# A state-space mixer with a quantized feed-forward layer: the preparation in a new order, with five weight scalings and a new form of normalization on POOL

## The reference

```python
# x: 4 x 512 x 512; ctx: 4 x 512 x 256
def mixer(ctx, z, ...):                      # per batch, E = 512 channels, 16 states
    x = einsum('ed,bld->bel', in_proj_w, ctx)
    u = silu(causal_conv4(x, conv_w) + conv_b)          # depthwise, 4 taps
    dt_lo, B, C = split(einsum('ke,bel->bkl', x_proj_w, u))
    delta = softplus(einsum('er,brl->bel', dt_proj_w, dt_lo) + dt_proj_b)
    state = state * exp(delta * A) + (delta * u) * B    # a scan over 512 steps
    y = sum_n(state * C) + D * u
    return (y * silu(z)).swapaxes(1, 2)

def bit_linear(x, w):                        # activations to 8 bits, weights to -1, 0, 1
    s = 1 / clip(mean(abs(w)), 1e-5)
    qw = clip(round(w * s), -1, 1) / s
    return einsum('bsh,oh->bso', activation_quant(x), qw)

x = x + mixer(ctx, layernorm(x))             # z is the normalized x
h = silu(bit_linear(layernorm(x), w_gate)) * bit_linear(layernorm(x), w_up)
x = x + bit_linear(rms_norm(h, ln_weight), w_down)
```

## Time and profile before

| what | value |
|---|---|
| time, median of 3 runs | 574.37 us (573.48 to 574.68) |
| profiled execution, its span (first to last instruction) | 572.7 us |
| busy: PE / DVE / ACT / POOL | 536.1 / 535.1 / 513.3 / 465.1 us |
| first scan starts | 93.42 us |
| DMA moved | 68.64 MB |

### The profile page before, as it was taken

The page is one execution under the profiler, slowest core; times in us unless marked ns, Lnnn a source line. Parts: engine busy times, 40 slices in busy tenths (PEclk is TensorE's granted clock), DMA queues, the critical chain, the costliest instruction groups (busy, mean ns, idle before and its releaser), DMA issues.

```text
span 572.7 us, 10285 instructions
## 1 busy us (share of the span) xinstructions
PE 536.1 (94%) x3667; PEld 403.2 (70%) x3684; DVE 535.1 (93%) x778; ACT 513.3 (90%) x757; POOL 465.1 (81%) x196
## 2 busy tenths in 40 slices
PE   5888988899999999999999889999899999999996
PEld 2335477799998999989899879998344444444443
DVE  3999988999999999999999999999999999999883
ACT  1899999999999999989999899999987878878784
POOL 4889364999999999999999999995757676675772
PEclk9999999999999999999999998999999999999999
DMA  9992591221111832126632257443544344533521
GB/s 279 408 390 76 201 323 36 55 58 57 56 56 56 191 105 93 56 65 123 165 99 63 59 129 188 137 154 97 83 78 96 76 101 84 110 84 71 106 55 74
DMA packets 62194, 68.64 MB, mean 120 GB/s; under 512 B 41137, under 2 KB 41137, under 8 KB 59969
## 3 DMA queue, kind: packets, MB, share of 16 engines
q1 hardware_dynamic: 59776, 63.59, 37.5%
q0 software_dynamic: 2368, 4.40, 4.8%
HBM read 50.02 MB, written 8.52 MB: 102 GB/s over the span
## 4 chain that ended last, share of the span: by engine, by line
PE 36%; ACT 24%; DVE 18%; POOL 9%; issue 7%; DMA 5%; SPq 0%; DVEq 0%; POOLq 0%
PE ps L1280 16%; ACT arena L697 11%; PE ps L1290 9%; POOL arena L475 9%; ACT arena L622 7%; DVE arena L840 5%; PE ps L1245 4%; PE ps L1229 4%; DMA arena<-c_rows 3%; DVE arena L929 3%; ACT arena L619 2%; PE ps L1232 2%; DVE bst_x L872 2%; DMA arena<-x 1%; DVE arena L864 1%
## 5 line engine op out<-in xcount | busy, mean ns | idle before, releaser
L475 POOL TENSOR_TENSOR arena<-arena 128x2048 f32<-128x2048 f32 x63 | 286.7, 4614 | 14.1 <-DVE arena L929 9.8
L929 DVE TENSOR_TENSOR_SCAN arena<-arena,ps 128x512 f32<-128x512 f32 x256 | 286.7, 1197 | 1.7 <-PE ps L1229 0.4
L697 ACT ACTIVATE arena<-arena,a_neg 128x512 f32<-128x512 f32 x256 | 164.8, 711 | 7.9 <-DVE arena L929 7.8
L1245 PE MATMUL ps<-ident,arena 128*128 128x128 f32 x1024 | 154.8, 274 | 5.9 <-POOL arena L475 3.7
L1245 PEld LDWEIGHTS ps<-ident,arena 128*128 128x128 f32 x1024 | 119.9, 141 | 9.7 <-POOL arena L475 5.3
L1280 PE MATMUL ps<-arena 128*128 128x512 bf16 x497 | 112.5, 379 | 3.6 <-DVE arena L1006 2.2
L1229 PE MATMUL ps<-arena 128*128 128x128 f32 x768 | 103.4, 278 | 3.9 <-DVE arena L929 3.8
L512 POOL TENSOR_TENSOR arena<-arena 128x1024 f32<-128x1024 f32 x30 | 71.0, 2366 | 39.9 <-DVE arena L1006 39.7
L622 ACT ACTIVATE arena<-arena,bT 128x512 f32<-128x512 f32 x160 | 102.0, 710 | 0.0
L1232 PE MATMUL ps<-ident,arena 128*128 128x128 f32 x640 | 96.0, 273 | 3.0 <-ACT arena L622 2.1
L1229 PEld LDWEIGHTS ps<-arena 128*128 128x128 f32 x768 | 94.5, 194 | 5.8 <-ACT arena L622 2.7
(11 more groups left out here) (122 smaller groups left out, 574.8 us busy)
## 6 DMA issues: line engine op xcount, KB each, us to landing
arena<-w_all SPq DMA_DIRECT2D x16, 1024.0 KB, 9.2
arena<-c_rows SPq DMA_DIRECT2D x64, 256.0 KB, 3.3
arena<-x SPq DMA_DIRECT2D x4, 1024.0 KB, 16.0
w_ternary<-arena SPq DMA_DIRECT2D x8, 512.0 KB, 4.1
arena<-w_ternary SPq DMA_DIRECT2D x8, 512.0 KB, 4.8
arena<-x POOLq DMA_DIRECT2D x4, 1024.0 KB, 10.6
out<-arena SPq DMA_DIRECT2D x16, 256.0 KB, 2.0
arena<-ctx_t SPq DMA_DIRECT2D x4, 512.0 KB, 14.0
```

What stands on the lines that cost most here:

```text
L475: nc.gpsimd.tensor_tensor(hs[:, k % RING, :, :], hs[:, k % RING, :, :], c_bc[:, s:s + 1, :].to_broadcast([P, KE, L]), ALU.mult).then_inc(S ...
L697: nc.scalar.activation(dA[:, s, i, :], delta_u[:, b, 0, i, :], ACT.Exp, scale=a_neg[:, i, n:n + 1]).then_inc(S["dA_ready"], 1)
L929: nc.vector.tensor_tensor_scan(out=hs[:, k % RING, i, :], data0=dA[:, k % 2, i, :], data1=ps[:, 4 + i, :], initial=0.0, op0=ALU.mult, op1= ...
L1245: last = mm(ps[:, c, i * P:(i + 1) * P], hs[:, k % RING, i, c * P:(c + 1) * P], ident[:], start=(n == 0 and i == 0), stop=(n == DS - 1), i ...
```

## The change

- POOL normalizes x by adding minus the mean (a new small instruction makes it) and multiplying, in place of subtract and multiply. The skip products get a second operation, plus 0.0.
- POOL scales five weight tiles, all of w_gate and (1, 1); ACT scales the other three. ACT sums eleven of twelve tiles (seven before), DVE one.
- w_down's tiles are loaded first, summed, and then overwritten by w_up's, each load of w_up waiting for one sum. w_gate is unchanged in place. du's memory is now where the context was, so `du(b)` waits no more for cuts and stores; it waits for delta, for all context products (b < 2) or for the turns of du(b - 2).
- All eight cuts are on DVE. ACT's one cut goes.
- Batches are worked in the order 3, 1, 0, 2 (convolution) and 1, 3, 0, 2 (x). The table of PSUM bank pairs, UNIT_AT, is written out, and so are the orders that the semaphores count in.
- PE begins with 12 keep_warm products; of the 27 between the preparation's products 6 stay.

```diff
-        du_s = part(128, 16).rearrange("p (s k l) -> p s k l", s=2, k=KE)
+        du_s = part(96, 16).rearrange("p (s k l) -> p s k l", s=2, k=KE)
-        W_AT = ((128, 136, 144, 152), (64, 72, 80, 88), (96, 104, 96, 104))
+        W_AT = ((128, 136, 144, 152), (64, 72, 80, 88), (64, 72, 80, 88))
...
+        def du_inputs(eng, b):
+
+            hold(eng, *both(unit_read, "dt", b))
+            if b < 2:
+                eng.wait_ge(S["in_proj_done"], NB * 2)
+            else:
+                hold(eng, *both(unit_full, "du", b - 2))
...
             def load_weight(w, k):
+                if w == 1:
+                    sp.wait_ge(down_summed[k], 1)
...
             def x_power(b):
-                pool.wait_ge(S["x_var"], b + 1)
-                nc.gpsimd.tensor_tensor(rstd_x[:, b, :], var_x[:, b, :], mhalf[:, 0:KE],
-                                        ALU.pow).then_inc(S["x_rstd"], 1)
-                pool.wait_ge(S["x_rstd"], b + 1)
+                pool.wait_ge(S["x_var"], ORDER["x"].index(b) + 1)
+                own.done(nc.gpsimd.tensor_scalar(minus_mean[:, b, :], mv_x[:, b, :, 0], -1.0, 0.0, ALU.mult, ALU.add))
+                own.done(nc.gpsimd.tensor_tensor(rstd_x[:, b, :], var_x[:, b, :], mhalf[:, 0:KE], ALU.pow))
+                own.wait()
...
-                    nc.gpsimd.tensor_scalar(row, row, mv_x[:, b, k, 0:1], rstd_x[:, b, k:k + 1], ALU.subtract,
+                    nc.gpsimd.tensor_scalar(row, row, minus_mean[:, b, k:k + 1], rstd_x[:, b, k:k + 1], ALU.add,
                                             ALU.mult).then_inc(S["x_normed"], 1)
...
+            def scale_weight(w, k):
+                pool.wait_ge(S["w_inv_ready"], w + 1)
+                pool.wait_ge(S["dve_consts"], 2)
+                nc.gpsimd.tensor_scalar(w_full(W_AT[w][k]), w_full(W_AT[w][k]), winv[:, w:w + 1], magic[:], ALU.mult,
+                                        ALU.add).then_inc(w_scaled[w][k], 1)
...
             def du(b):
-                pool.wait_ge(S["delta_ready"], delta_count(b, 1))
-                if b < 2:
-                    pool.wait_ge(S["w_staged"], (4, 7)[b])
-                    pool.wait_ge(wq_stored[0][b], 16)
-                else:
-                    pool.wait_ge(S["duT_psum"], (b - 2) * 2 + 2)
+                du_inputs(pool, b)
                 nc.gpsimd.tensor_tensor(du_s[:, b % 2, :, :], delta_u[:, b, 0, :, :], delta_u[:, b, 1, :, :],
-                                        ALU.mult).then_inc(S["du_ready"], 1)
+                                        ALU.mult).then_inc(du_ready[b], 1)
...
+            scale_weight(0, 3)
+            x_power(1)
+            scale_weight(0, 1)
...
```

More of the change, by code:

```diff
@@ L155, in mixer_ffn @@
         bst_x, mv_x = sb("bst_x", [P, KE, 6]), sb("mv_x", [P, NB, KE, 2])
-        var_x, rstd_x = sb("var_x", [P, NB, KE]), sb("rstd_x", [P, NB, KE])
+        var_x, rstd_x, minus_mean = [sb(n, [P, NB, KE]) for n in ("var_x", "rstd_x", "minus_mean")]
         bst, mv = sb("bst", [P, 6]), sb("mv", [P, 2])
@@ L197, in mixer_ffn, with summed @@
         LAST = NB * DS - 1
-        ACT_SUMMED, DVE_SUMMED = (5, 7, 7), (0, 1, 5)
-        DVE_CUT, ACT_CUT = ((0, 0), (0, 3), (0, 1), (0, 2), (1, 1), (1, 0), (1, 2)), ((1, 3),)
+        du_ready = [sem(f"du_ready{b}") for b in range(NB)]
+        w_summed = [sem("w0_summed"), sem("w1_summed")]
+        down_summed = [sem(f"down_summed{k}") for k in range(4)]
+        w_scaled, w_staged = [[[sem(f"w{w}_{what}{k}") for k in range(4)] for w in range(2)]
+                              for what in ("scaled", "staged")]
+        def summed(w, k):
+            return down_summed[k] if w == 2 else w_summed[w]
         FFN_STEPS = range(TILES)
@@ L469, in _ @@
             du(3)
+            pool.wait_ge(S["consts_loaded"], 16 * 2)
+            for k in range(KE):
+                nc.gpsimd.tensor_scalar(skip[:, k, :], ident[:], dsk[:, k:k + 1], 0.0, ALU.mult,
+                                        ALU.add).then_inc(S["skip_ready"], 1)
             def product(k):
@@ L615, in inputs_of @@
                 if n == 0:
[L616 removed]
+                    hold(act, *both(unit_read, "du", b))
                 for i in range(KL):
@@ L668, in _ @@
             silu_z(0, 1)
+            keep_bT(1)
             scale_weight(1, 3)
@@ L694, in _ @@
                         inputs_of(k)
+                    if k < 2:
+                        hold(act, *both(unit_full, "du", 2 + k))
                     for i in range(KE):
@@ L861, in cut_weight @@
             def cut_weight(w, k):
[L862 removed]
+                dve.wait_ge(w_scaled[w][k], 1)
                 out = w_cut(W_AT[w][k])
                 nc.vector.tensor_scalar(out, halves(w_full(W_AT[w][k])), MAGIC, 1.0, ALU.subtract,
[L865 to L867 removed]
+                                        ALU.min).then_inc(S["dve_steps"], 1)
+                own.n += 1
+                own.wait()
+                nc.vector.tensor_scalar(out, out, -1.0, None, ALU.max).then_inc(w_staged[w][k], 1)
             def x_stats(b):
@@ L1095, in take @@
             def take(kind, b, h):
-                before = UNIT_USERS.index((kind, b, h)) - 3
-                if before >= 0:
-                    hold(pe, *unit_read(*UNIT_USERS[before]))
+                users = list(UNIT_AT)
+                before = [u for u in users[:users.index((kind, b, h))] if UNIT_AT[u] == UNIT_AT[kind, b, h]]
+                if before:
+                    hold(pe, *unit_read(*before[-1]))
                 return two(kind, b, h)
@@ L1156, in total @@
             def total(w):
-                hold(pe, "w_summed_act", ACT_SUMMED[w], "w_summed", DVE_SUMMED[w])
+                if w < 2:
+                    pe.wait_ge(w_summed[w], 4)
+                else:
+                    for k in range(4):
+                        pe.wait_ge(down_summed[k], 1)
                 mm(ps[:, 7, 0:4], ones[:], wstat[:, w * 4:w * 4 + 4], start=True, stop=True).then_inc(S["w_total"], 1)
@@ L1186, in _ @@
             delta_in(0, 1)
+            project(1)
             pe.wait_ge(S["bT_ready"], 1)
             total(1)
-            project(1)
             delta_in(1, 1)
+            delta_in(3, 0)
             delta_in(2, 0)
-            delta_in(3, 0)
             delta_in(2, 1)
             delta_in(3, 1)
+            pe.wait_ge(S["w_added"], 2)
+            turn_xdbl(1)
             turn_z(0, 0)
             turn_z(0, 1)
-            pe.wait_ge(S["w_mean_done"], 2)
-            turn_xdbl(1)
             turn_du(0, 0)
-            keep_warm(3)
+            turn_du(0, 1)
             turn_z(1, 0)
             turn_z(1, 1)
-            keep_warm(3)
-            turn_du(0, 1)
+            turn_du(1, 0)
+            turn_du(1, 1)
+            pe.wait_ge(S["bT_ready"], 2)
+            total(2)
             turn_z(2, 0)
             turn_z(2, 1)
-            turn_du(1, 0)
-            keep_warm(2)
-            turn_du(1, 1)
             turn_z(3, 0)
```

236 lines of the change are left out of this document (109 added, 127 removed), and 12 rows, old and new, of tables (ORDER, UNIT_AT, UNIT_USERS).

## The result

The changed kernel takes 586.85 us (median of 4 runs, 586.13 to 587.39) beside 573.92 for the kernel before on the same chip: ratio 1.0211, 95% interval 1.0190 to 1.0232. It is slower by 2.1%; 588.1 was forecast. The profiled execution has a span of 585.5 us, 12.8 more than before.

The account below looks back on a forecast made before the run. It took DVE's almost gapless preparation work before the first scan as the bound: scan at 107.1 instead of 93.4, 13.7 later; 572.7 + 13.7 + 1.7 = 588.1 us, own range 583.5 to 592.5, 8 in 10 range 567 to 592.5.

Parts of the forecast that it names:

- The fixed part: From the first scan to the end, instructions unchanged: taken as fixed at 479.3 us.
- step 1: Start of the preparation: reordered loads and DVE's first sums make winv of w_gate ready at 30.2 us.
- step 2: ACT's work up to the last silu of u: winv of w_up ready at 59.3, du(0) allowed at 59.0.
- step 3: POOL's new forms: 2.3 us a weight tile, 0.6 a row of x; upper end 8.3 and 2.07.
- step 4: Cuts on DVE and du on POOL block each other and take turns; last copies end at 105.1; chance 0.50.
- step 5: PE's turns after standing some 14 us run at half speed: 0 to 3.5 us, 2.0 taken.
- no collision: Rival: cuts run beside du; first scan at 87.7, total 568.7 us, range 567 to 571; chance 0.23.
- DVE goes first: Rival: DVE keeps the port and POOL stands; first scan at 100.0, total 581.0 us; chance 0.16.
- POOL slow: Rival: POOL's new form is slow and delays du(0); total 604 or 637 us; chance 0.10.
- a sign of being wrong: In the changed kernel's profile: the prediction is wrong if POOL's scales take over 3 us.
- du(0) near 59: Sign expected on POOL in the changed kernel's profile: du(0) starts near 59 us, with scales of about 2.3.

Follow-up runs that it names:

- early_front_3us: The changed kernel with the convolution's weights loaded ahead of the first x and 14 more idle matmuls ahead of project(0): 585.35 us, ratio 1.0188.
- old_norm_form: The changed kernel with x normalized on POOL by subtract and multiply, as in the kernel before: 599.22 us, ratio 1.0431.
- warm_turns_13us: The changed kernel with 55 idle matmuls on PE between turn_z(1,0) and turn_z(1,1): 584.29 us, ratio 1.0169.
- du_held: The changed kernel with all du held on POOL until seven cuts are staged, scale(1,1) and cut(1,2) moved ahead: 582.82 us, ratio 1.0142.
- du_on_dve: The changed kernel with the four du products on DVE, POOL keeping only scale(1,1) in that stretch: 577.92 us, ratio 1.0051.

## Why the prediction was right, step by step

- *The fixed part.* 478.1 us from the first scan on, 479.3 forecast: right to 1.2 us, and within the spread of the runs. But the prediction came to its first scan by DVE's path alone (du(3), the last cut, its store, the last copies), and the changed kernel's chain of waits does not pass there. From DVE's first copy at 88.05 it goes over PE's turns and ACT's silus of z to ACT's last table load and the first exponentials:

```profile
98.31 1.08 PE ps L1170 x8
...
99.41 1.94 ACT arena L599 x2
...
101.36 1.28 ACT L708
...
103.23 2.56 ACT arena L726 x4
```

  The table load starts 12.5 us later than before (88.86), the span is 12.8 longer, the first scan 13.97 later. The prediction has no sum for ACT behind the first copies with the block; that both paths end so close to each other was luck. How much the last copies' wait for the store adds to the time was not tried.
- *Loads and first sums (step 1).* winv of w_gate was ready at 31.0 (30.2).
- *ACT up to du(0) (step 2)* was mis-sized: winv of w_up came at 62.4 and du(0) at 62.2, where the text has 59.3 and 59.0. I had priced project at full clock, 3.65, while project(0), behind 3.98 us of standing, took 6.12 at a granted clock of 0.59 and ACT waited 1.80 for it. early_front_3us takes that back and du(0) comes 1.8 us earlier. There ACT's third softplus ends at 60.3 and POOL's last row of x at 60.4, so the other 1.4 us lie on both engines; they weren't followed further.
- *POOL's form (step 3).* 2.05 us a tile and 0.77 a row, 2.3 and 0.6 forecast; with 8.3 and 2.07, the other bound, the kernel would have been slower still, as old_norm_form shows for the rows alone. The estimate from the Trainium skill's page "GPSIMD Engine Reference", section 3.1, 1.8 us a tile, is 0.25 too low; for subtract and multiply, 2,076 ns for 512 elements, it stays wrong.
- *Turns (step 4)* were right in kind: alternating passes, a one-input scale that blocks as du does (a cut's second pass took 2.44 beside it), PE held at turn_z(1,1) for 13.4 us, du(3) across the last cut, the last copies behind a store. In size the stretch from du(0) to the first scan was 45.2 us and not 48.1: six cuts were done 25.9 us behind du(0)'s start (27.3), the first copies waited for no store (0.6), and the last store landed 3.4 us behind its cut instead of 4.75 (1.3). The last cut ended 1.9 behind du(3) instead of 2.2. du(3) came 0.9 later behind the copies than forecast, clock included.
- *Clock (step 5).* 2.0 us forecast; 2.0 between warm_turns_13us and the changed kernel, 1.1 if the stretch of early_front_3us is taken instead.

So +13.97 us at the first scan where 13.7 were forecast: 3.2 us of lateness at du(0) and 2.9 us too much for the turns nearly cancel. That the total is better than its parts is luck.

The rivals: *no collision* falls with the first four cut rows. *DVE goes first* did not happen here, though DVE does keep ahead in other runs (below). *POOL slow* would have needed over 2.95 us a tile; the one scale that took 3.03, over the 3 us that the prediction gave as a sign of being wrong, took 2.05 and a wait of 1.0 for a cut pass. du(0) near 59 is the one sign that did not come.

## What to carry to other kernels

A wait that an engine sits out may be what keeps it from colliding with another engine: before you delete one, look for a row where the two did meet, and compare its end with the other's end, not its length with a mean. Work that excludes itself across two engines is summed, not overlapped, so holding one part back does not bring its time back (du_held); what can help is to put one part into a form or on an engine where it doesn't collide (at the first scan du on DVE brought 10 us, the cuts with one operand in PSUM 3.8) or into a stretch where the other engine has nothing to do. And where an engine has stood, price the next matmuls at the clock that the trace grants them.

## What the runs showed of the hardware that was not expected

- Two pairs of operations that do the same arithmetic differ by a factor of 2.7 on POOL: a row of 512 by subtract and multiply takes 2,076 ns, by add and multiply 766 to 770, and a tile of 2,048 by multiply and add 2,050. A multiply with no second operation takes 609 ns for 128 elements, with an added zero 374.
- The turns are not always strict. In the changed kernel a waiting pass came in between du(0) and the scale; in old_norm_form a pass stood through du(1) and du(2), 9.98 us. On the other side, in du_on_dve, POOL's scale stood through a du and the pass behind it on DVE. DVE's timeline of that run:

```profile
62.34 2.29 DVE L908 TENSOR_TENSOR arena<-arena 128x2048 f32<-128x2048 f32 x1
64.55 1.22 DVE L884 TENSOR_SCALAR arena<-arena 128x2048 bf16<-128x2048 f32 x1
65.81 2.36 DVE L888 TENSOR_SCALAR arena<-arena 128x2048 bf16<-128x2048 bf16 x1
```

And POOL's, of the same run:

```profile
62.52 5.10 POOL L471 TENSOR_SCALAR arena<-arena,winv,magic 128x2048 f32<-128x2048 f32 x1 [2.05 <-DVE winv L879]
```

The scale ends at 67.62, so its 2.05 us began near 65.57, about when the first pass ended (65.77). In both cases the engine that kept on had its next instruction free to start, while between a cut's two passes DVE waits for the first to end. That alone does not decide: in the changed kernel POOL's next instruction was free to start at 66.7 and at 69.7 too (winv stood at 62.4, the delta of batch 1 by 66.5), and a pass came in between both times. What decides stays open.
